# Two 32-head attentions: the queries of two heads from seven block products in place of eight

## The chip, the cores and the metric

The kernel is one program on one core of a Trainium2 chip (trn2). The metric is its time on the device in microseconds (us), lower is better. Engines: TensorE (PE, matrix products; PEld is its loading of weights), VectorE (DVE), ScalarE (ACT), GpSimd (POOL) and SyncE (SP, which issues the transfers here).

## The reference

A decoder of four layers on x of 16 batches by 64 tokens by 512 (1024 tokens in all), float32 throughout. The change touches the attention (`L3_attn`) and the cross attention (`L3_xattn`) of the last layer. Both have 32 heads of 128, in 8 groups of 4 heads that share a key and a value head:

```python
q = (hidden_states @ Wq.T).reshape(bsz, q_len, N_HEADS, HEAD_DIM).transpose(0, 2, 1, 3)   # L3_attn
q = q * cos + _rotate_half(q) * sin
q = (latents @ Wq).reshape(bsz, q_len, HEADS, HEAD_DIM).transpose(0, 2, 1, 3)             # L3_xattn
q = rms_norm(q, q_norm_w)
```

Then follow scores with the keys, softmax, the product with the values and the output product `@ Wo`, which is added to x. In `L3_attn` the scores are causal; in `L3_xattn` there are 128 keys per batch (64 of the context, 64 of the latents) and no mask.

## The kernel before, in words

The stages run one after the other; the last ones are `l2f`, `l3a` (`L3_attn`, kind "rope"), `l3x` (`L3_xattn`, kind "rms") and `l3f`. `l3a` and `l3x` are both built by `stage_gqa` (L600). The normalised tokens lie transposed in `kvT[:, k, 1, :]`: 128 features of block k (k = 0 to 3) by 1024 tokens. In `l3a` they are there when the stage begins; `l3x` makes them itself first (`front`). The half `kvT[:, k, 0, :]` held the context and is read by no one in these two stages.

**The work of a group.** Each stage goes through 8 groups of 4 heads. For each group TensorE makes: the keys (`keys`, L805, two blocks of 512 tokens, each 4 products of 128 by 128 weights with 512 tokens, summed over k in one bank of `pj`); the queries (`queries`, L812, 4 heads by 2 blocks, 4 products each, so 32); the scores of each head (`scores`, L864, 16 small products); transposes of the softmax's result (`turns`, L886); the values (`values`, L796, two blocks); the weighted values (`attend`, L901, four parts); and the output (`out`, L922, 8 tiles of 128 tokens with 4 products each). In the trace one float32 product stands as two records, so a product of 512 columns has two rows MATMUL 128x512. `l3x` also has, on TensorE, the sums of squares of keys (`key_sums`) and queries (`pair_sums` of two heads, `pair_turn`), for the rms norm.

**Banks and who empties them.** Keys, queries and values pass through the two banks of `pj`, by turns. In `l3a` ScalarE copies each block to `raw` (L988), and VectorE rotates it with four operations (`turn`, L1131 to L1145): a product with the cosine, two half-high products with the sine, and a sum into `qT` or `kT`. In `l3x` ScalarE squares the block (L1028) and copies it to `qT` (L1029); VectorE does nothing to queries. The softmax (`softmax`, L1167) is on VectorE, five large operations and a small one, with the exponential on ScalarE between (L1056). VectorE also adds each output tile to x (L1196).

**What sets the order.** Each engine has its own queue, written out by hand, and takes its instructions in that order; semaphores hold an instruction until its inputs are ready. The order is in `opening`, `group` and `closing` of each engine (TensorE: L939 to L979; ScalarE: L1071 to L1113; VectorE: L1242 to L1270). `group(n)` holds the queries of group n, from head 1 on, with the output of group n - 1 between them, and towards its end the keys and the first head's queries of group n + 1. `over_groups` (L698) writes TensorE's groups out one by one, and makes loops (`Fori`) of two groups on ScalarE and VectorE. SyncE loads weights of group n (`load`, L714) when the outputs of group n - 2 are done. GpSimd only copies key weights in `l3a` (L781), and helps in the norm of the next stage at the end. In `l3x` VectorE also unpacks weights of the next stage between the softmaxes (`unpack`, `dequantise`, L1199): part 0 is 32 small operations, part 1 four, and each later part two or three picks, a pick being L1224 and L1227. The first group does 8 parts, groups 1 to 6 four each, the last none.

## Time and profile before

| | us |
|---|---|
| median of 3 runs | 4217.38 |
| lowest and highest | 4216.12, 4219.28 |
| the profiled execution | 4217.35 |
| its span, first to last instruction | 4215.4 |
| mean granted clock of TensorE | 0.965 |
| `l3a`, first product to last group's last value block | 2714.0 to 3319.4 |
| `l3x`, the same | 3390.1 to 4094.8 |

A row of a timeline has the start in us from the span's start, the length, the engine, the line, the instruction and how many such in one go; in brackets is the idle time before it and what released it. Lengths of products are pipelined: the next one starts before the end that a row shows. A row of a group by line has the busy time, the mean of one in ns, and the idle time before it. Idle time of TensorE counts, since it is the engine that is nearly always busy; idle time of another one costs only where TensorE waits for it.

### The profile page before, as it was taken

Reading aid. Unit: us, or ns where it says so; the run is one execution under the profiler, and the core shown is the slowest. Engines: PE = TensorE matmul, PEld = TensorE weight load, DVE = VectorE, ACT = ScalarE, POOL = GpSimd, SP = SyncE. Lnnn points to the kernel's source line nnn. Section 1 sums busy time; section 2 is a strip of 40 time slices with the busy share of each in tenths; the row PEclk is TensorE's granted clock in tenths of the full one; section 3 lists DMA queues with packets and bytes.
Section 4 is the critical chain, followed back from the end, with each engine's and each line's share of the span. In section 5 each row is a group of like instructions: output and inputs, shape, how many; then the busy total and the mean of one; then the engine's idle time right before and its main releaser. Section 6 shows DMA issues by size and latency. Waiting matters only on the chain. (4 is left out here: it accounts for less than half of the span.)

```text
span 4215.4 us, 50580 instructions
## 1 busy us (share of the span) xinstructions
PE 3910.7 (93%) x18762; PEld 2088.9 (50%) x18762; DVE 2173.2 (52%) x3802; ACT 1425.1 (34%) x2570; POOL 313.7 (7%) x288
## 2 busy tenths in 40 slices
PE   8788989998989999998999889699999999999997
PEld 3333334554455555554447654355555455555554
DVE  0887765552247333333547548766556455444443
ACT  3777745553223211111113334222111133222332
POOL 1011001211001100000000111000000000000000
PEclk9899999999989999999999989899999999999998
DMA  5111121111100432311001022100010021111100
GB/s 187 45 40 35 53 76 33 33 31 58 40 33 16 178 113 103 116 54 73 1 13 55 1 101 58 64 21 21 21 40 21 1 67 36 36 35 40 65 6 23
DMA packets 133945, 215.20 MB, mean 51 GB/s; under 512 B 42576, under 2 KB 95056, under 8 KB 123104
## 3 DMA queue, kind: packets, MB, share of 16 engines
q1 hardware_dynamic: 133728, 212.19, 14.5%
q8 instruction: 151, 2.47, 0.2%
q14 instruction: 66, 0.54, 0.0%
HBM read 168.12 MB, written 44.04 MB: 50 GB/s over the span
## 5 line engine op out<-in xcount | busy, mean ns | idle before, releaser
L930 PE MATMUL l3a_po<-l3a_wo,l3a_cT 128*128 128x512 f32 x512 | 230.5, 603 | 3.5 <-ACT l3a_cT L1067 3.2
L436 PE MATMUL l1x_pj<-kvT,l1x_wq 128*128 128x512 f32 x512 | 228.3, 599 | 0.7 <-ACT kvT L240 0.7
L481 PE MATMUL l1x_po<-l1x_wo,l1x_cT 128*128 128x512 f32 x512 | 226.3, 596 | 1.2 <-issue 1.2
L819 PE MATMUL l3x_pj<-kvT,l3x_wq 128*128 128x512 f32 x512 | 225.5, 593 | 0.0
L819 PE MATMUL l3a_pj<-kvT,l3a_wq 128*128 128x512 f32 x512 | 224.9, 592 | 0.0
L577 DVE TENSOR_TENSOR x<-x,l1x_po 128x512 f32<-128x512 f32 x64 | 43.9, 687 | 267.1 <-PE l1x_po L481 267.1
L930 PEld LDWEIGHTS l3a_po<-l3a_wo,l3a_cT 128*128 128x128 f32 x512 | 95.5, 191 | 121.6 <-issue 110.9
L819 PEld LDWEIGHTS l3a_pj<-kvT,l3a_wq 128*128 128x128 f32 x512 | 95.5, 190 | 111.5 <-issue 111.4
L481 PEld LDWEIGHTS l1x_po<-l1x_wo,l1x_cT 128*128 128x128 f32 x512 | 95.7, 192 | 111.0 <-issue 111.0
L819 PEld LDWEIGHTS l3x_pj<-kvT,l3x_wq 128*128 128x128 f32 x512 | 95.5, 190 | 111.4 <-issue 111.4
L436 PEld LDWEIGHTS l1x_pj<-kvT,l1x_wq 128*128 128x128 f32 x512 | 94.6, 190 | 110.2 <-issue 107.2
L194 POOL TENSOR_TENSOR norm_rstd<-norm_half,minus_half 128x1 f32<-128x1 f32 x70 | 41.6, 595 | 1367.4 <-DVE norm_half L189 1367.4
L930 PE MATMUL l3x_po<-l3x_wo,l3x_cT 128*128 128x512 f32 x256 | 117.6, 603 | 0.7 <-issue 0.7
L1196 DVE TENSOR_TENSOR x<-x,l3a_po 128x512 f32<-128x512 f32 x56 | 38.4, 686 | 149.7 <-PE l3a_po L930 149.7
L930 PE MATMUL l3x_pc<-l3x_wo,l3x_cT 128*128 128x512 f32 x256 | 115.1, 592 | 0.0
L531 ACT COPY l1x_cT<-l1x_pa 128x512 f32<-128x512 f32 x64 | 34.4, 589 | 238.5 <-PE l1x_pa L470 238.5
L1631 ACT ACTIVATE l0a_signs<-l0a_lowest_a,l0a_scalars 128x1376 uint16<-128x1376 uint16 x68 | 98.0, 1442 | 47.9 <-DVE l0a_lowest_a L1755 47.1
L1740 DVE TENSOR_SCALAR_CACHE_REDUCE l0a_keep<-l0a_keep,l0a_scalars 128x1376 uint16<-128x1376 uint16 x64 | 105.3, 1646 | 3.2 <-DVE l0a_scalars L1746 1.1
L2627 PE MATMUL l1f_ph<-l1f_w,l1f_xT 128*128 128x448 f32 x256 | 104.6, 558 | 0.0
L2651 PE MATMUL l1f_po<-l1f_w,l1f_hT 128*128 128x512 f32 x224 | 101.6, 599 | 1.9 <-ACT l1f_hT L2694 1.9
L1740 DVE TENSOR_SCALAR_CACHE_REDUCE l0a_keep<-l0a_a,l0a_scalars 128x1376 uint16<-128x1376 uint16 x60 | 98.7, 1646 | 4.2 <-DVE l0a_scalars L1746 2.1
L1503 PE MATMUL l0a_pg<-kvT,fill_wk 128*128 128x512 f32 x160 | 74.5, 618 | 25.1 <-ACT l0a_s L1580 13.5
(532 smaller groups left out, 7633.7 us busy)
## 6 DMA issues: line engine op xcount, KB each, us to landing
l1x_kb<-l1x_keys SPq DMA_DIRECT2D x32, 512.0 KB, 4.7
l1x_vb<-l1x_values SPq DMA_DIRECT2D x32, 512.0 KB, 3.5
l1x_keys<-l0a_kv SPq DMA_DIRECT2D x40, 256.0 KB, 2.0
fill_wk<-in_L_xattn_Wk SPq DMA_DIRECT2D x8, 1024.0 KB, 5.7
kvT<-in_L_xattn_Wv SPq DMA_DIRECT2D x8, 1024.0 KB, 5.7
l1x_values<-l0a_kv SPq DMA_DIRECT2D x32, 256.0 KB, 2.3
l1x_wq<-in_L_xattn_Wq SPq DMA_DIRECT2D x8, 1024.0 KB, 5.0
l1x_sbias<-in_L_xattn_bias SPq DMA_DIRECT2D x8, 1024.0 KB, 6.8
```

The source lines that it names most:

```text
L194: self.nc.gpsimd.tensor_tensor(self.rstd[:, t:t + 1], self.half[:, t:t + 1], self.m.minus_half[:, 0:1], ALU.pow).then_inc(self.root_ready, 1)
L436: mm = pe.matmul(pj[:, j, :], wq[:, u, k, h * DH:(h + 1) * DH], m.kvT[:, k, 1, 512 * j:512 * (j + 1)], start=k == 0, stop=k == KC - 1)
L481: mm = pe.matmul(po[:, t % 2, :], cT[:, u, h, t * P:(t + 1) * P], wo[:, u, h, :], start=h == 0, stop=h == GH - 1)
L577: nc.vector.tensor_tensor(m.x[:, t, :], m.x[:, t, :], po[:, t % 2, :], ALU.add).then_inc(added, 1)
L819: mm = pe.matmul(pj[:, j, :], wq[:, u, k, h * DH:(h + 1) * DH], m.kvT[:, k, 1, 512 * j:512 * (j + 1)], start=k == 0, stop=k == KC - 1)
L930: mm = pe.matmul(outs[t % 2][:, :], cT[:, h, t * P:(t + 1) * P], wo[:, u, h, :], start=h == 0, stop=h == GH - 1)
L1196: nc.vector.tensor_tensor(m.x[:, t, :], m.x[:, t, :], outs[t % 2][:, :], ALU.add).then_inc(added, 1)
L1503: mm = pe.matmul(banks[b], wk[:, k, h * DH:(h + 1) * DH], m.kvT[:, k, 0, 512 * j:512 * (j + 1)], start=k == 0, stop=k == KC - 1)
L1631: ins = nc.scalar.activation(signs[:, :], words, ACT.Sign, bias=at[:, :], scale=-1.0, accum_out=total[:, :])
L1740: nc.vector.tensor_scalar(below, words, found[:, :], 0.0, ALU.is_lt, ALU.add, accum_out=cnt[:, :]).then_inc(link, step.next())
L2627: mm = pe.matmul(ph[:, c % 2, 0:CH1], f.xT[:, u, k, :], w1[:, k, c * CH1:(c + 1) * CH1], start=k == 0, stop=k == KC - 1)
L2651: mm = pe.matmul(f.po[:, :], hT[:, j, :], w2[:, j, :], start=j == 0, stop=j == HC1 - 1)
```

## The change

The queries of two heads (a pair p, two pairs per group) are a product of weights with blocks (features 0 to 255 and 256 to 511) by (head, head) and tokens with blocks (features) by (tokens 0 to 511, 512 to 1023). Before, this takes 8 block products, each of 2 products of 128 by 128 by 512. After, it takes 7 (`step` k = 1 to 7, 2 products each, 14 steps per group) and sums:

- **sums of tokens**, once per stage: four VectorE operations of 128 by 1024 (`fold_tokens`), into `kvT[:, i, 0, :]`.
- **sums of weights**, per pair: four GpSimd operations of 128 by 256 (`mix`), into `ws`; 8 per group, both stages.
- **sums of results**, per pair: ScalarE copies steps 1, 4 and 5 to SBUF (`saved`), VectorE adds steps 2, 3, 6 and 7 from the bank to something kept (`summed`), and three additions in SBUF (`join`, `join_both`) finish it, on GpSimd in `l3a` and on VectorE in `l3x`. In `l3x` ScalarE squares the finished blocks from SBUF (`square`) where it squared the bank.

The order is written anew: each step of two products alternates between the banks and waits for the bank's last reader; steps 1 to 6 of the first pair come ahead of the group that they belong to, and the steps of the second pair stand between parts of the output. VectorE's softmax is split into `scaled`, `shift` and `weighed`, with other work between; the last part of head 3 moves into the next group. In `l3x` VectorE unpacks four parts in each of the 8 groups: 4 parts fewer in the first, and 4 in the last, where there were none. All engines' groups are written out one by one, without loops.

```diff
-    NU = NV + NK + 8
+    NU = NV + NK
...
-        raw = st.sb("raw", [P, 2, 512])
+        raw = st.sb("raw", [P, 6 if rope else 2, 512])
+        ws = st.sb("ws", [P, 4, 2, DH])
...
+                def mix(n, p):
...
+                    if p == 0:
+                        pool.wait_ge(w_loaded[u], 8 * loads * (n + 2 - u))
+                        if n:
+                            pool.wait_ge(q_step, step_at(n - 1, 1, 6) + 2)
+                    else:
+                        pool.wait_ge(q_step, step_at(n, 0, 6) + 2)
+                    nc.gpsimd.tensor_tensor(ws[:, 0], low2, high2, ALU.add).then_inc(mixed, 1)
+                    pool.wait_ge(mixed, mixed_at(n, p, 0) + 2)
+                    nc.gpsimd.tensor_tensor(ws[:, 1], ws[:, 0], low, ALU.subtract).then_inc(mixed, 1)
+                    nc.gpsimd.tensor_tensor(ws[:, 2], low, low2, ALU.subtract).then_inc(mixed, 1)
+                    pool.wait_ge(mixed, mixed_at(n, p, 1) + 2)
+                    nc.gpsimd.tensor_tensor(ws[:, 3], high, ws[:, 1], ALU.subtract).then_inc(mixed, 1)
+                def join(n, p):
...
+                    nc.gpsimd.tensor_tensor(keep(1), keep(0), keep(1), ALU.add).then_inc(q_joined, 1)
...
+                    nc.gpsimd.tensor_tensor(keep(0), keep(0), keep(2), ALU.add).then_inc(q_joined, 1)
...
+                    nc.gpsimd.tensor_tensor(query(1, 1), keep(1), keep(2), ALU.add).then_inc(q_joined, 1)
...
+                    for c in range(2):
+                        block = wq[:, u, c if k == 1 else 2 + c, (2 * p + (k == 7)) * DH:(2 * p + (k == 7) + 1) * DH]
+                        weights = block if k in (1, 2, 7) else ws[:, {3: 1, 4: 0, 5: 2, 6: 3}[k], c, :]
+                        stream = {1: tokens(c, 0), 2: tokens(2 + c, 0), 3: fold(1, c), 4: fold(0, c), 5: fold(2, c),
+                                  6: tokens(2 + c, 1), 7: fold(3, c)}[k]
+                        mm = pe.matmul(pj[:, p if k % 2 else 1 - p, :], weights, stream, start=c == 0, stop=c == 1)
+                    mm.then_inc(q_step, 1)
```

TensorE's group, before and after (its waits: `values(0)` and `values(1)` of a group wait for `summed` of steps 6 and 7 of pair 1; `scores(n, u, 0)` in `l3a` waits for the rotation of block 1 of head 0, `scores(n, u, 1)` for that of head 1; the step after a step waits for its bank's reader):

```diff
                 def opening():
...
-                    queries(0, 0, 0)
+                    for k in range(1, 7):
+                        step(0, 0, 0, k)
...
-                    queries(n, u, 1)
+                    step(n, u, 1, 1)
+                    step(n, u, 0, 7)
                     scores(n, u, 0)
-                    pair_sums(n, 0)
                     if behind:
                         turns(n - 1, 3)
+                    pair_sums(n, 0)
+                    step(n, u, 1, 2)
                     pair_turn(n, 0)
-                    queries(n, u, 2)
+                    step(n, u, 1, 3)
                     if behind:
                         attend(n - 1, 0)
-                    scores(n, u, 1)
+                    step(n, u, 1, 4)
                     if behind:
...
-                        rest_of_out(n - 1, 1 - u)
+                        out(n - 1, 1 - u, 0)
+                        attend(n - 1, 1)
+                        out(n - 1, 1 - u, 1)
+                    scores(n, u, 1)
+                    step(n, u, 1, 5)
...
                     for j in range(NV):
                         values(n, u, j)
+                    pair_sums(n, 1)
                     turns(n, 0)
-                    queries(n, u, 3)
+                    pair_turn(n, 1)
                     scores(n, u, 2)
-                    pair_sums(n, 1)
                     turns(n, 1)
-                    pair_turn(n, 1)
                     if more:
                         all_keys(n + 1, 1 - u)
-                        queries(n + 1, 1 - u, 0)
+                        for k in range(1, 5):
+                            step(n + 1, 1 - u, 0, k)
                     scores(n, u, 3)
+                    if more:
+                        step(n + 1, 1 - u, 0, 5)
+                        step(n + 1, 1 - u, 0, 6)
                     turns(n, 2)
```

VectorE's order after (`add` in the parts named is of group n - 1, left out in the first group):

```diff
+                    fold_tokens()
                     all_keys(0, 0)
-                    queries(0, 0)
+                    summed(0, 0, 2)
+                    rotate(0, 0, 0)
+                    summed(0, 0, 3)
+                    join(0, 0)
+                    summed(0, 0, 6)
+                    join_both(0, 0)
+                    rotate(0, 0, 1)
...
+                    summed(n, 0, 7)
+                    rotate(n, 1, 1)
+                    summed(n, 1, 2)
+                    scaled(n, 0)
+                    summed(n, 1, 3)
+                    shift(0)
+                    rotate(n, 1, 0)
...
+                    weighed(n, 0)
+                    rotate(n, 2, 0)
...
+                    scaled(n, 1)
+                    join(n, 1)
+                    shift(1)
...
+                    join_both(n, 1)
+                    weighed(n, 1)
+                    summed(n, 1, 6)
+                    rotate(n, 3, 1)
...
+                    summed(n, 1, 7)
+                    rotate(n, 2, 1)
...
+                    rotate(n, 3, 0)
...
+                    for i in range(3):
+                        unpack(n, i)
+                    scaled(n, 2)
+                    shift(2)
+                    weighed(n, 2)
+                    unpack(n, 3)
                     if more:
                         all_keys(n + 1, 1 - u)
-                        queries(n + 1, 0)
-                    softmax(n, 3)
-                    unpack(lap, u, 3)
+                        summed(n + 1, 0, 2)
+                        rotate(n + 1, 0, 0)
+                        summed(n + 1, 0, 3)
+                    scaled(n, 3)
...
```

## Rows read from the trace of the kernel before

**Rows 1.** The page: span, and busy time of each engine.
```profile
span 4215.4 us, 50580 instructions
...
PE 3910.7 (93%) x18762; PEld 2088.9 (50%) x18762; DVE 2173.2 (52%) x3802; ACT 1425.1 (34%) x2570; POOL 313.7 (7%) x288
```

**Rows 2.** Stretches: from:to, length, busy us PE, PEld, DVE, ACT, POOL, clock, DMA, GB/s.
```profile
2722.60:2777.27 54.67, 54.67 (x301) 30.32 (x300) 44.29 (x68) 11.43 (x20) 1.70 (x2) 1.00 0.05 22
2945.00:3022.00 77.00, 76.15 (x375) 40.38 (x374) 43.86 (x67) 15.01 (x28) 1.00 (x1) 1.00 0.08 28
...
4102.00:4135.00 33.00, 20.88 (x121) 14.11 (x120) 12.54 (x12) 8.83 (x15) 0.00 (x0) 0.64 0.00 1
```

**Rows 3.** Groups by line: busy us, mean ns, then idle before and its releaser.
```profile
L819 PE MATMUL l3a_pj<-kvT,l3a_wq 128*128 128x512 f32 x512 | 224.9, 592 | 0.0
L930 PE MATMUL l3a_po<-l3a_wo,l3a_cT 128*128 128x512 f32 x494 | 222.8, 604 | 3.5 <-ACT l3a_cT L1067 3.2
...
L1224 DVE TENSOR_SCALAR l3x_pick<-l3x_code,l3x_lut 128x512 f32<-128x512 f32 x60 | 29.0, 484 | 4.4 <-DVE l3f_wl L1227 0.5
```

**Rows 4.** Timeline of TensorE, middle group of `l3a`: start, length, instruction, idle before.
```profile
2962.17 7.13 PE L930 MATMUL l3a_po<-l3a_wo,l3a_cT 128*128 128x512 f32 x16
...
2996.41 7.03 PE L819 MATMUL l3a_pj<-kvT,l3a_wq 128*128 128x512 f32 x16
```

**Rows 5.** Timeline of VectorE, `l3a`: rotation, softmax, rotation; addition from PSUM; two sine products twice.
```profile
2949.93 0.69 DVE L1139 TENSOR_TENSOR l3a_part<-l3a_raw,l3a_cosq 128x512 f32<-128x512 f32 x1 [0.19 <-DVE l3a_qT L1145]
...
2952.70 0.68 DVE L1175 SCALAR_TENSOR_TENSOR l3a_sc<-l3a_pS,causal 128x512 f32<-128x512 f32 x1
...
2957.09 0.68 DVE L1139 TENSOR_TENSOR l3a_part<-l3a_raw,l3a_cosq 128x512 f32<-128x512 f32 x1
...
2965.91 0.69 DVE L1196 TENSOR_TENSOR x<-x,l3a_po 128x512 f32<-128x512 f32 x1 [2.34 <-PE l3a_po L930]
...
3011.98 1.70 DVE L1142 TENSOR_TENSOR l3a_part<-l3a_raw,l3a_sink 64x512 f32<-64x512 f32 x2
...
3015.33 1.40 DVE L1142 TENSOR_TENSOR l3a_part<-l3a_raw,l3a_sink 64x512 f32<-64x512 f32 x2
```

**Rows 6.** Timeline of VectorE at the start of `l3a`.
```profile
2720.15 0.69 DVE L1139 TENSOR_TENSOR l3a_part<-l3a_raw,l3a_cosk 128x512 f32<-128x512 f32 x1 [11.78 <-ACT l3a_raw L988]
```

**Rows 7.** Timeline of TensorE, first group of `l3a`: its first value block.
```profile
2745.64 7.41 PE L802 MATMUL l3a_pj<-l3a_wvf,kvT 128*128 128x128 f32 x64
```

**Rows 8.** Timeline of VectorE, start of `l3x`: one softmax lies between these two.
```profile
3419.17 1.22 DVE L1179 TENSOR_TENSOR l3x_sc<-l3x_pS,l3x_rq 128x1024 f32<-128x1024 f32 x1 [16.54 <-ACT l3x_rq L1046]
...
3426.66 3.40 DVE L1207 TENSOR_SCALAR l3x_bits<-l3x_packed 128x64 int32<-128x64 int32 x32
```

**Rows 9.** Timeline of TensorE, start of `l3x`: first queries, first value block.
```profile
3399.96 13.90 PE L819 MATMUL l3x_pj<-kvT,l3x_wq 128*128 128x512 f32 x32
...
3427.31 7.41 PE L802 MATMUL l3x_pj<-l3x_wv,kvT 128*128 128x128 f32 x64
```

**Rows 10.** Timeline of TensorE, last group of `l3a`: first and last transposes.
```profile
3319.35 0.60 PE L897 MATMUL l3a_px<-ident,l3a_sc 128*128 128x128 f32 x4
...
3339.28 1.12 PE L897 MATMUL l3a_px<-ident,l3a_sc 128*128 128x128 f32 x4 [3.28 <-DVE l3a_sc L1191]
```

**Rows 11.** Timeline of TensorE, last group of `l3x`: first and last transposes.
```profile
4094.75 1.04 PE L897 MATMUL l3x_px<-ident,l3x_sc 128*128 128x128 f32 x8
...
4123.18 1.97 PE L897 MATMUL l3x_px<-ident,l3x_sc 128*128 128x128 f32 x8 [5.52 <-DVE l3x_sc L1191]
```

**Rows 12.** GpSimd, an addition of two tiles, by line.
```profile
L289 POOL TENSOR_TENSOR x<-x,l2a_ob 128x512 f32<-128x512 f32 x8 | 12.7, 1582 | 165.0 <-ACT l2a_ob L281 165.0
...
L289 POOL TENSOR_TENSOR x<-x,l1f_ob 128x512 f32<-128x512 f32 x8 | 10.1, 1268 | 218.3 <-ACT l1f_ob L281 218.3
```

**Rows 13.** Timeline of GpSimd, `l3a`: the same copy in two groups.
```profile
2930.72 0.62 POOL L781 COPY l3a_wk<-l3a_wkf 128x512 f32 x1 [79.99 <-PE l3a_pj L810]
3012.15 1.00 POOL L781 COPY l3a_wk<-l3a_wkf 128x512 f32 x1 [80.81 <-PE l3a_pj L810]
```

More of the change, by code:

```diff
@@ L979, in closing @@
                     rest_of_out(GROUPS - 1, 1)
-                over_groups(pe, opening, group, closing, unrolled=True)
+                over_groups(opening, group, closing)
             @block.scalar
@@ L1115, in _ @@
                 nc.scalar.preload_act_table_set("natural_log_exp_and_others")
-                over_groups(act, opening, group, closing)
+                over_groups(opening, group, closing)
             @block.vector
@@ new lines, in summed @@
+                def summed(n, p, k):
+                    dve.wait_ge(q_step, step_at(n, p, k) + 2)
+                    if k < 6:
+                        dve.wait_ge(q_saved, saved_at(n, p, 1) + 2)
+                    else:
+                        dve.wait_ge(q_joined, joined_at(n, p, "four" if k == 6 else "five") + 2)
+                    if k == 3:
+                        dve.wait_ge(q_summed, summed_at(n, p, 2) + 2)
+                    if rope and pair(n, p) and k != 3:
+                        dve.wait_ge(rotated, turn_q(n if p else n - 1, (1 if k == 7 else 0) + (0 if p else 2), 1 if k == 6 else 0) + 2)
+                    dst, src = {2: (query(0, 0), keep(0)), 3: (keep(0), keep(0)), 6: (query(0, 1), keep(1 if rope else 0)),
+                                7: (query(1, 0), keep(0 if rope else 1))}[k]
+                    nc.vector.tensor_tensor(dst, src, pj[:, p if k % 2 else 1 - p, :], ALU.add).then_inc(q_summed, 1)
@@ new lines, in rotate @@
+                def rotate(n, h, j):
+                    if rope:
+                        if h % 2 and j:
+                            dve.wait_ge(q_joined, joined_at(n, h // 2, "both") + 2)
+                        else:
+                            dve.wait_ge(q_summed, summed_at(n, h // 2, {(0, 0): 2, (0, 1): 6, (1, 0): 7}[h % 2, j]) + 2)
+                        if pair(n, h // 2):
+                            dve.wait_ge(s_ready, GH * n + h - 2 + 2)
+                        turn(turn_q(n, h, j), query(h, j), qT[:, h % 2, 512 * j:512 * (j + 1)], cosq, sinq)
@@ L1241, in opening @@
                 def opening():
+                    if rms:
+                        dve.wait_ge(front.copied, T + 1)
+                    fold_tokens()
                     all_keys(0, 0)
-                    queries(0, 0)
-                def group(n, u, behind, more, lap):
-                    chain.at(4 * TURN + per * n)
-                    queries(n, 1)
-                    softmax(n, 0)
-                    unpack(lap, u, 0)
-                    queries(n, 2)
-                    if behind:
-                        add(n - 1)
-                    softmax(n, 1)
-                    unpack(lap, u, 1)
-                    queries(n, 3)
-                    softmax(n, 2)
-                    unpack(lap, u, 2)
+                    summed(0, 0, 2)
@@ L1258, in group @@
                     if more:
                         all_keys(n + 1, 1 - u)
-                        queries(n + 1, 0)
-                    softmax(n, 3)
-                    unpack(lap, u, 3)
-                    assert chain.n == (per if more else per - 4 * TURN), (chain.n, per)
+                        summed(n + 1, 0, 2)
+                        rotate(n + 1, 0, 0)
+                        summed(n + 1, 0, 3)
+                    scaled(n, 3)
+                    if more:
+                        join(n + 1, 0)
@@ L1272, in closing @@
                     ahead.shifts(dve, T - 1, 0, T - 1)
-                over_groups(dve, opening, group, closing)
+                over_groups(opening, group, closing)
     ahead.done((T - 1, T))
```

357 lines of the change are left out of this document (245 added, 112 removed).

## The prediction

> **What bounds the kernel now.** I read the page first: TensorE is busy 93% of the span and no other engine over 52% [rows 1]. Then the stretches of the two changed stages. TensorE is busy for all of the first 54.7 us in `l3a`, and for 76.2 of 77.0 us of a middle stretch, at full granted clock, where VectorE has 43.9 us of work. In the first stretch VectorE has 44.3 of 54.7 us [rows 2]: that is 81%, since no output products stand beside its work there. By line, the queries of `l3a` are 512 records that never waited [rows 3]. So TensorE's own work sets the time, and an instruction of it that goes is worth its full price as long as the others keep up. The exceptions are the two ends, where the last softmaxes run with nothing beside them; one such stretch has TensorE busy 20.9 of 33 us at a mean clock of 0.64 [rows 2].
>
> All sums are against the profiled execution, 4217.35 us: a span of 4215.4 and 2.0 around it. The median of the runs is 4217.38, the same.
>
> **What goes.** 16 records of a query block last 7.03 us, of which some 0.16 is the last one's drain [rows 4]: 0.429 us each. A product of 512 columns is two records, 0.857 us. Per group 32 query products become 28, so 3.43 us go; over 16 groups 64 products, **54.9 us**. They do not go evenly: six steps in place of one head's queries are made ahead (10.3 us for 6.86, so 3.43 more in the opening), the seven groups after it save 3.43 each, and the last group, with nothing to make ahead, saves 6.86. Up to the last group's value blocks that is 20.6 us per stage; the rest is in the last group's end, worked out below.
>
> **What comes, and what covers it.**
> Hand-over of a bank: an output block of two units starts at 2962.17, its first unit of 8 records ends 3.43 later at 2965.60 [rows 4], and VectorE's addition from the bank starts at 2965.91 and takes 0.69 [rows 5]. So a bank is free again 0.3 + 0.7 + some 0.05 = 1.05 us after its step. The other bank's step takes 1.71. If the reader is idle, nothing is lost; what counts is whether VectorE's queue is late.
>
> Middle groups, `l3a`. VectorE gets 8 additions of 0.69 more, about 50 us of work in some 74. Where it could be late is the end of a group. A rotation takes 2.77 us and a whole softmax 4.39 [rows 5]. From the start of the keys (call it 0): key block 0 ends at 3.4 and is copied at 4.2, rotated until 7.1; block 1 is copied at 7.7 and rotated until 10.5; `summed` 2 until 11.2, the first rotation until 14.0, `summed` 3 until 14.7. TensorE wants bank for step 4 at 12.0 and for step 5 at 14.8 (steps 1 to 4 until 13.7, scores 1.1): just in time. Step 6 ends at 18.2, and the next user of its bank is step 1 of the next pair, with only 0.45 us of transposes between: it waits 1.05 - 0.45 = **0.6 us** per group, 4.2 in seven. In the middle of a group the outputs (3.43 us each) stand between steps and VectorE had idle stretches of 2 to 4 us before each addition: I cost the other hand-overs at nothing. Without that cover each would cost up to the 0.69 of its addition.
> Middle groups, `l3x`. The same place has 0.9 us of transposes, but `summed` 6 stands behind `scaled` 3 and two joins: 0.4 us, 2.8 in seven.
> An old wait goes: the outputs waited 3.2 us in `l3a` for ScalarE's copies [rows 3], which now have a step between; one of them, 1.1, is in the closing and stays. Gain 2.1.
>
> First group, `l3a`. Here nothing is beside VectorE. Its first rotation starts at 2720.15, after 11.8 us idle [rows 6]; the four sums of tokens (5 us, an estimate: twice 1024 columns' worth of the 0.69 for 512, less the fixed part) fit into that and cost nothing. From there to `summed` 6 of pair 1, which frees the bank for the first values, it has 7 rotations (19.6 with gaps), 7 additions from the bank (5.0), two softmaxes of which one exponential is now covered (8.1), and waits of 0.5 for key block 1 and 3.5 for step 6: 36.7 us, until 2756.9. TensorE would be there at 2745.64 [rows 7] + 3.43 (14 steps for 3 heads' queries) = 2749.1. Stall **8 us**; I take 8.2 with the hand-over. After it both go on as in a middle group.
>
> First group, `l3x`. `summed` 6 of the opening is late behind the joins: 1.2 us. Then the first `scaled` starts at 3419.17 [rows 8] plus two steps more (nine for two heads' queries, 1.7) plus 1.2 = 3422.1. From there VectorE has two softmaxes of 7.49 each [rows 8], `summed` 3 and 6 and two joins, four times 0.7: 17.8, until 3439.9. TensorE would be at the values at 3427.31 [rows 9] + 3.43 + 1.2 = 3431.9. Stall 8.0, with the other 1.2 and less the 0.7 us that it waited in the turning of sums before: **8.5**.
>
> Last group, `l3a`. From its first to its last transposes there are 19.9 us now [rows 10], of which 6.86 are queries. After: transposes 0.5, scores 1.1, and two softmaxes of 4.39 back to back: 10.5. Gain **9.4** (the queries' 6.86, and VectorE no longer behind the last rotations).
> Last group, `l3x`: 28.4 us now [rows 11]. After: 5.0 to 5.4 of transposes, sums and scores, two softmaxes 15.0, and the unpacking that now stands between them, two picks of 0.48 [rows 3] + 0.69: 2.4. That is 22.4 to 22.8; gain **6.0**.
>
> Clock. After the 3.2 and 5.5 us of idle in the last groups the same eight transposes took 1.97 us against 1.04 [rows 11], in the stretch with mean clock 0.64. That is the lower level of 1.2 GHz. The stalls in the first groups are of that size, and most of the time with a slow TensorE falls into the wait itself; I take 2 us for `l3a`, 3 for `l3x`, between 0 and 10 together.
>
> GpSimd. An addition of 512 columns there takes 1.27 to 1.58 us [rows 12]. The joins of `l3a` have 2.5 us each before someone waits, the weights' sums more; free. But they run beside VectorE: the key weights' copy took 1.00 us in one group and 0.62 in another [rows 13], and the two sine products beside the longer one took 1.70 us, against 1.40 [rows 5]. So 1 us of GpSimd costs VectorE some 0.3. Six joins and eight sums of weights (half the size) are some 14 us per group: VectorE loses 4 us, in its slack except in the first group, where I take 2. Bounds: 0, and 1 us for 1 us (rival 2).
>
> Written-out loops, more semaphores, ScalarE's three copies for four: nothing; TensorE's queue is written out already and its queries never waited [rows 3].
>
> **Sum.** `l3a`: -20.6 - 9.4 - 2.1 + 8.2 + 4.2 + 2 + 2 = -15.7. `l3x`: -20.6 - 6.0 + 8.5 + 2.8 + 3 = -12.3. Together -28.0: **4189.4 us**.
>
> **Rivals.**
> 1. All cover holds: the first groups don't stall (their waits overlap better than I chain them). Then 30.0 + 26.6 + 2.1 go: 4158.7. For it: VectorE was 19% idle in the first stretch [rows 2]. Against: its new work there, 7 additions and two more rotations before the values, is more than that idle. Chance 0.10.
> 2. GpSimd and VectorE share a path to memory. The trace has 0.3 us lost per us with a one-input copy; with two inputs on both sides it could be all of it. Then VectorE has 50 + 14 = 64 us in 74, the first group of `l3a` stalls some 8 us more, and each middle group 1 us: 28.0 - 8 - 7 + 2 saved are left, 15: about 4202. Chance 0.16.
> The Trainium skill, "GPSIMD Engine Reference", Specifications, has a rule that speaks for this: GpSimd's SBUF interfaces are shared with VectorE, with contention for VectorE instructions that have two SBUF inputs. Rotations are such. By that rule, taken as strict turn-taking, the time would be this rival's; the row's 0.3 us agrees with the rule in kind and is milder in size.
> 3. Slower: the chain at the end of a group, `summed` 2, rotation, `summed` 3, join, `summed` 6, before step 1 of the next pair. I found it in time by 0.1 us at step 5. If each of its links comes 0.5 us later, or a copy of ScalarE stands behind an exponential, TensorE waits twice or three times there. 28.0 us over 14 middle groups is 2.0 us per group, the point from which nothing is gained; at 4 us per group the time is 4217.35 + 28 = 4245. Against: ScalarE is busy 20% in these stretches [rows 2], and one late link eats only its own slack. Chance 0.07.
> 4. The forecast, with both first groups stalling 4 to 12 us each: 0.67.
>
> **How the numbers follow.** The likeliest case gives 4189.4. Its own bounds: no clock cost, no cost from GpSimd, half of the 16.7 us stalls, -15 in all; a clock cost of 10 and middle waits doubled, +12. With rival 2, and without most of rival 3 and of rival 1: **4168 to 4208**. A measurement of this kernel can tell about 0.2%, 8.4 us, from no change. Faster than 4208.9: the forecast, rival 1 and most of rival 2, 0.87. Within 8.4 us: 0.07. Slower than 4225.8: 0.06.
>
> **What would show it.** TensorE's query records: 896 in place of 1024, still 0.43 us each. In the first group of each stage, an idle time of TensorE before the first value block (line of `values`), released by VectorE's `summed`, 3 to 8 us. Before step 1 of pair 1, 0.4 to 0.6 us per group. Last transposes of `l3a` some 10.5 us, of `l3x` some 22.5 us after the first. The sine products of `l3a` longer than 0.70 us beside GpSimd. I am wrong if middle groups (77 us stretches) show TensorE idle by more than 2 us each, or if the first value blocks don't wait.

## The result and the profile after

The changed kernel takes 4209.64 us (median of 20 runs, 4206.61 to 4215.01), the kernel before beside it 4216.28 (20 runs, 4212.38 to 4219.28): a ratio of 0.9986, 95% interval 0.998 to 0.9993. It is faster by 6.6 us where 28 were forecast, and lies just outside the range of 4168 to 4208. The profiled execution took 4207.24 us.

The page of the changed kernel, span and first section, beside [rows 1]:
```profile
span 4205.3 us, 50002 instructions
...
PE 3867.1 (92%) x18634; PEld 2066.0 (49%) x18634; DVE 2328.0 (55%) x3986; ACT 1414.8 (34%) x2538; POOL 498.6 (12%) x464
```
The 128 records of the 64 products that go are gone (18762 to 18634). PE's busy time fell by 43.6 us and not by 54.9, so other records got longer. In the two first groups busy time is some 7 us longer than the products that went explain, at a granted clock of 0.92 where the kernel before has 0.96 and 1.00. In the groups behind them it is some 11 us longer at a granted clock of 1.00, so there it isn't the clock. (The tails and the other stages have some 7 us less.) Of the 43.6 us only some 10 arrived in the span of this execution. VectorE has 155 us more work, GpSimd 185.

The rest of the accounting is by start times in TensorE's timeline. A stage is cut at the first key block of its first group, of its second, and so on, and at the first and last transposes of the last softmaxes. Groups are counted from 0, so "keys 7" is the first key block of the last group. "Forecast" is the prediction's own sum put into these pieces: each group with 28 products for 32 is 3.43 shorter, and the last piece before the tail 3.43 longer, since no steps are left to make ahead.

| piece, us | before | after | change | forecast |
|---|---|---|---|---|
| `l3a`, first group (keys 0 to keys 1) | 47.90 | 58.59 | +10.7 | +8.8 |
| `l3a`, a middle group (six; mean before) | 80.96 | 79.69 | -1.3 | -3.1 |
| `l3a`, keys 7 to first last-group transposes | 71.7 | 77.57 | +5.9 | +3.7 |
| `l3a`, tail (first to last transposes) | 19.93 | 10.67 | -9.3 | -9.4 |
| `l3a`, all | 625.32 | 624.95 | **-0.4** | -15.7 |
| `l3x`, first group | 56.95 | 64.77 | +7.8 | +8.1 |
| `l3x`, a middle group (six) | 94.31 | 92.11 | -2.2 | -3.0 |
| `l3x`, keys 7 to transposes | 81.84 | 87.34 | +5.5 | +3.8 |
| `l3x`, tail | 28.42 | 21.44 | -7.0 | -6.0 |
| `l3x`, all | 733.1 | 726.19 | **-6.9** | -12.3 |

Both tails and the first group of `l3x` came as forecast, within 1 us. `l3a` as a whole gained nothing, and most of that is its middle groups. The two stages together gained 7.3 us, which agrees with the medians; the other 3 us between the two profiled executions lie ahead of `l3a`, where nothing was changed, and vary from run to run.

A middle group of `l3a`, end of the group before and start of its steps, in TensorE's timeline (start, length, engine, line, tiles, idle before and its releaser):
```profile
2784.28 3.70 PE L912 MATMUL l3a_pj<-kvT,l3a_ws 128*128 128x512 f32 x8
2787.82 0.60 PE L991 MATMUL l3a_px<-ident,l3a_sc 128*128 128x128 f32 x4
2788.76 3.70 PE L912 MATMUL l3a_pj<-kvT,l3a_wq 128*128 128x512 f32 x8 [0.34 <-DVE l3a_raw L1322]
2793.54 1.15 PE L977 MATMUL l3a_pS<-l3a_kT,l3a_qT 128*64 128x64 f32 x32 [1.08 <-DVE l3a_qT L1292]
2795.01 0.66 PE L991 MATMUL l3a_px<-ident,l3a_sc 128*128 128x128 f32 x4 [0.32 <-DVE l3a_sc L1390]
```
The first wait, 0.34, is the hand-over that was forecast (before `step` 1 of pair 1, behind `summed` 6). The second, 1.08, was not: the scores wait for the rotated queries of the first head. VectorE and GpSimd at that time:
```profile
2788.02 0.69 DVE L1322 TENSOR_TENSOR l3a_raw<-l3a_saves,l3a_pj 128x512 f32<-128x512 f32 x1 [1.48 <-PE l3a_pj L912]
2788.74 1.26 DVE L1286 TENSOR_TENSOR l3a_part<-l3a_raw,l3a_cosq 128x512 f32<-128x512 f32 x1
2790.03 2.23 DVE L1289 TENSOR_TENSOR l3a_part<-l3a_raw,l3a_sinq 64x512 f32<-64x512 f32 x2
2792.30 1.10 DVE L1292 TENSOR_TENSOR l3a_qT<-l3a_part 128x512 f32<-128x512 f32 x1
2793.32 0.67 DVE L1386 TENSOR_REDUCE l3a_tot<-l3a_sc 128x8 f32<-128x512 f32 x1
```
```profile
2788.19 1.27 POOL L828 TENSOR_TENSOR l3a_raw<-l3a_saves 128x512 f32<-128x512 f32 x1
2789.42 1.17 POOL L812 TENSOR_TENSOR l3a_ws<-l3a_wq 128x256 f32<-128x256 f32 x1
2790.66 1.06 POOL L814 TENSOR_TENSOR l3a_ws<-l3a_ws,l3a_wq 128x256 f32<-128x256 f32 x1
2791.69 1.17 POOL L815 TENSOR_TENSOR l3a_ws<-l3a_wq 128x256 f32<-128x256 f32 x1
2792.81 1.17 POOL L817 TENSOR_TENSOR l3a_ws<-l3a_wq,l3a_ws 128x256 f32<-128x256 f32 x1
```
A rotation of 2.77 us [rows 5] takes 4.6 here, beside GpSimd's last join and its weight sums. The addition before it, with one input in PSUM, and the reduction behind it, with a single input, keep their 0.69 and 0.67 beside the same engine.

The ends of these rows (start plus length) show how the two engines stand in each other's way. The join ends at 2789.46, the cosine product at 2790.00, the first weight sum at 2790.59; then the second weight sum at 2791.72, the sine products at 2792.26, the third weight sum at 2792.86, VectorE's sum at 2793.40 and the last weight sum at 2793.98. Each end is 0.54 to 0.60 us behind the one before it, which is the other engine's. The one step of 1.13 holds the first of the two sine products, whose own end the row doesn't show. So each instruction gets going only when the other engine's is done.

The first value blocks wait as forecast:
```profile
2747.85 1.90 PE L977 MATMUL l3a_pS<-l3a_kT,l3a_qT 128*64 128x64 f32 x32 [3.72 <-DVE l3a_qT L1292]
2758.58 8.85 PE L869 MATMUL l3a_pj<-l3a_wvf,kvT 128*128 128x128 f32 x64 [2.65 <-DVE l3a_raw L1322]
...
3436.47 9.50 PE L869 MATMUL l3x_pj<-l3x_wv,kvT 128*128 128x128 f32 x64 [7.95 <-DVE l3x_qT L1322]
```
Behind the waits the same 64 products take 8.85 and 9.50 us against the 7.41 of [rows 7], at a mean granted clock of 0.82 and 0.76: part of them ran at the lower level of 1.2 GHz.

### The profile page after: what moved, and what is told of

Its sections match the earlier page's. It is cut to its first block and busy times, and to the rows that moved or that the text cites. A ratio compares the mean times of both kernels' runs of the same rounds, so it can differ in the third digit from the quotient of the medians.

```text
span 4205.3 us, 50002 instructions
## 1 busy us (share of the span) xinstructions
PE 3867.1 (92%) x18634; PEld 2066.0 (49%) x18634; DVE 2328.0 (55%) x3986; ACT 1414.8 (34%) x2538; POOL 498.6 (12%) x464
## 5 line engine op out<-in xcount | busy, mean ns | idle before, releaser
L912 PE MATMUL l3a_pj<-kvT,l3a_ws 128*128 128x512 f32 x256 | 121.6, 608 | 1.8 <-DVE l3a_saves L1322 1.6
L912 PE MATMUL l3x_pj<-kvT,l3x_ws 128*128 128x512 f32 x256 | 119.4, 601 | 0.0
L2425 POOL TENSOR_TENSOR l0x_q<-l0x_q,l0x_qi 128x512 f32<-128x512 f32 x64 | 65.4, 1044 | 306.9 <-DVE l0x_qi L2713 306.9
L1289 DVE TENSOR_TENSOR l3a_part<-l3a_raw,l3a_sinq 64x512 f32<-64x512 f32 x128 | 96.3, 752 | 4.0
L1728 PE MATMUL l0a_pg<-l0a_wg,l0a_xT 128*128 128x512 f32 (+1 forms) x192 | 81.8, 585 | 16.1 <-issue 13.5
```

The source lines that it names most:

```text
L912: mm = pe.matmul(pj[:, p if k % 2 else 1 - p, :], weights, stream, start=c == 0, stop=c == 1)
L1289: nc.vector.tensor_tensor(batches(part[low:low + S, 1, :]), batches(src[high:high + S]), s, ALU.mult).then_inc(link, chain.next())
L1728: mm = pe.matmul(dst[:, c, 0:k], f.xT[:, n % 2, kc, :], w[:, kc, o:o + k], start=kc == 0, stop=kc == KC - 1)
L2425: nc.gpsimd.tensor_tensor(qv, qv, qi[:, c % 2, b, :].unsqueeze(2).to_broadcast([P, XH, XD]), ALU.mult).then_inc(q_done, 1)
```

## The experiments

Theory after the result: GpSimd's additions in `l3a` take from VectorE's two-input instructions just where those decide. Rivals: VectorE's own new work is too much, with or without GpSimd; or the cost is in TensorE's clock and in its seams, the places where it changes from products of one tile size to products of another, where no wait shows.

**One stage at a time.** `l3a`, then `l3x`, by the function of the kernel before:
```diff
-        stage_gqa(nc, m, "l3a", "rope", ...
+        stage_gqa_8(nc, m, "l3a", "rope", ...
```


> The kernel after with l3a as before (eight products), l3x as after. It splits the measured 6.6 us between the stages. By the account of the two traces l3a gained nothing (0.3 us from its first key product to its last output) and l3x gained 7 to 9: then this run is 7 us faster than before, 4209, the same as the changed kernel. Rival: both gained half, as the prediction had it in kind (15.7 and 12.3 of 28): then it is some 3 us faster than before, 4213.

> The kernel after with l3x as before, l3a as after. If l3a gained nothing, this is the time of before, 4216 within 2 us, and its l3a lasts 653 us from the first key product to the last output, as in both traces. Rival (equal shares): 3 us faster than before.

Measured: with the old `l3a` 4208.67 us (11 runs), ratio to before 0.9985, interval 0.9976 to 0.9994: as fast as the changed kernel. With the old `l3x` 4218.15 (11 runs), 1.0005, 0.9996 to 1.0014: no gain at all. So the whole gain is `l3x`'s, as the table says, and what `l3a` lost it lost inside itself.

**The weight sums taken out of the place where they stand.** `ws` gets two buffers in `l3a`, and both pairs' sums are made before the group:
```diff
-        ws = st.sb("ws", [P, 4, 2, DH])
+        ws = st.sb("ws", [P, 2 if rope else 1, 4, 2, DH])
...
-                    mix(n, 1)
+                    if rms:
+                        mix(n, 1)
...
                         mix(n + 1, 0)
+                        if rope:
+                            mix(n + 1, 1)
```


> In l3a the sums of weights get two buffers, and those of both pairs are made together before the group, when VectorE has little to do; l3x unchanged. Theory GpSimd (its work beside VectorE lengthens the rotation that scores 0 wait for): in the changed kernel the rotation beside three joins and four sums of weights took 5.1 us in place of 2.8. Without the sums beside it, its sine products go back from 2.23 to 1.4 and its last sum from 1.10 to 0.69, the wait of 1.08 us before scores 0 falls to under 0.2 and the 0.32 before the transposes goes: 1.2 us in each of 7 groups and 1 to 2 us in the first, 9 us, 4200. Theory seams (TensorE loses 0.1 us at each change between large and small products): nothing changes, 4209. Theory VectorE (too much work of its own): nothing in middle groups either, waits stay.

Measured: 4203.4 us (7 runs), ratio 0.9969, 0.9958 to 0.998. The last three middle groups took 78.46 to 78.50 us, 1.2 less. `l3a` in all took 619.39, 5.6 less than in the changed kernel, where the expectation had 9. The first group took 59.85, 1.3 more and not 1 to 2 less: it waits as long in all (10.2 us for 10.1), but more of it comes early, with the second pair's sums in the opening. The 8 records behind the wait for `summed` 3 took 5.37 us, at a granted clock of 0.68, for 3.67 at 1.00. (The rotation of 5.1 us in the expectation is 4.6 by the rows above, and one join runs beside it, not three.) The waits of TensorE between 2870 and 3270 us, in middle groups (waited for, us in total, times, longest), first of the changed kernel:
```profile
PE l3a_pS L977 <- DVE l3a_qT L1292: 5.4, 5, 1.1
PE l3a_pj L912 <- DVE l3a_raw L1322: 1.7, 5, 0.3
PE l3a_px L991 <- DVE l3a_sc L1390: 1.6, 5, 0.3
```
and of this experiment:
```profile
PE l3a_pj L918 <- DVE l3a_raw L1328: 2.1, 6, 0.3
PE l3a_px L997 <- DVE l3a_sc L1396: 1.2, 5, 0.2
PE l3a_pj L918 <- DVE l3a_saves L1328: 0.8, 2, 0.5
```
The same additions in another place: the wait of the scores is gone. That of the transposes fell only from 0.3 to 0.2. What counts is beside what GpSimd's work stands.

**The joins of `l3a` on VectorE.** 
```diff
-                    if rope:
-                        join(n, 0)
...
+                    dve.wait_ge(q_saved, saved_at(n, p, 5) + 2)
+                    dve.wait_ge(q_summed, summed_at(n, p, 3) + 2)
+                    nc.vector.tensor_tensor(keep(1), keep(0), keep(1), ALU.add)...
```


> In l3a the three joins of a pair go from GpSimd to VectorE, where l3x has them; the sums of weights stay on GpSimd as in the changed kernel. Theory GpSimd: the sums of weights start earlier, since they no longer stand behind the joins, but may still run beside the same rotation; the joins cost VectorE 6 x 0.7 us per group more. Step 1 of pair 1 waits for summed 6, which now stands behind two joins on VectorE: its wait grows from 0.34 to some 0.7 us, that of scores 0 falls from 1.08 to some 0.5. Together within 2 us of the changed kernel per stage, and the first group 2 us slower, as VectorE sets it: 4208 to 4212. Rival (joins were the costly part of GpSimd's work): waits before scores 0 vanish, 4202.

Measured: 4217.16 us (11 runs), ratio 1.0004, 0.9995 to 1.0013; a middle group 80.96. A miss, some 8 us slower than the changed kernel, and not the 4208 to 4212 that were expected. Its waits in the same stretch:
```profile
PE l3a_pj L909 <- DVE l3a_raw L1319: 8.5, 5, 1.7
PE l3a_pS L974 <- DVE l3a_qT L1289: 4.7, 5, 1.0
PE l3a_px L988 <- DVE l3a_sc L1387: 1.6, 5, 0.3
```
The wait before `step` 1 rose from 0.3 to 1.7, and not to 0.7: two joins of 0.69 now stand in VectorE's queue before `summed` 6. There the links of the chain are in series, and taking them off VectorE is right. The wait of the scores stayed, since the weight sums still stand beside the rotation.

**Nearly all of GpSimd's additions left out** in `l3a`. This kernel leaves out sums that the result needs; it only prices them.
```diff
+                cols = 1 if rope else DH
...
+                    low, high, low2, high2 = (w[:, :, 0:cols] for w in (low, high, low2, high2))
...
-                    nc.gpsimd.tensor_tensor(keep(1), keep(0), keep(1), ALU.add)
+                    nc.gpsimd.tensor_tensor(keep(1)[:, 0:1], keep(0)[:, 0:1], keep(1)[:, 0:1], ALU.add)
```


> In `l3a` GpSimd's weight sums and joins work on one column each, in the same order and behind the same waits; nearly all of these sums are left out. Theory (GpSimd's additions lengthen VectorE's turns beside them, and their own length makes the second head late): the wait before `scores` 0 goes (from 1.08 us per middle group to 0), VectorE's two longest turns fall from 2.23 to about 1.4 us and from 1.10 to 0.7, and a middle group of `l3a` takes 78.2 in place of 79.7. Rival (VectorE's own chain of copies, folds and sums is what is late, with or without GpSimd): the wait stays within 0.3 us of what it is and the group at 79.4 to 79.8. Second rival (the clock and the changes of shape take it): the same, with no wait to speak of at either place.

Measured: 4192.91 us (one run, so the readings are by start times in its trace). A middle group takes 77.94, the first group 53.74 (4.9 less), `l3a` in all 607.89, 17.1 less. The same place in VectorE's timeline:
```profile
2787.01 0.69 DVE L1331 TENSOR_TENSOR l3a_raw<-l3a_saves,l3a_pj 128x512 f32<-128x512 f32 x1 [1.48 <-PE l3a_pj L921]
2787.73 0.69 DVE L1295 TENSOR_TENSOR l3a_part<-l3a_raw,l3a_cosq 128x512 f32<-128x512 f32 x1
2788.45 1.40 DVE L1298 TENSOR_TENSOR l3a_part<-l3a_raw,l3a_sinq 64x512 f32<-64x512 f32 x2
2789.89 0.69 DVE L1301 TENSOR_TENSOR l3a_qT<-l3a_part 128x512 f32<-128x512 f32 x1
```
and in TensorE's:
```profile
2787.75 3.70 PE L921 MATMUL l3a_pj<-kvT,l3a_wq 128*128 128x512 f32 x8 [0.34 <-DVE l3a_raw L1331]
2791.38 1.15 PE L986 MATMUL l3a_pS<-l3a_kT,l3a_qT 128*64 128x64 f32 x32
```
The rotation is 2.8 us again and the scores don't wait, with all of VectorE's own new work still there: the first rival falls. The second falls as well: nothing in TensorE's order was changed, and what was missing came back. The hand-over's 0.34 stays, as it should: the one join that `summed` 6 needs was done 2.5 us before it in the changed kernel too.

**Only the weight sums left out**, in both stages (again sums that the result needs):
```diff
+                    low, high, low2, high2 = (w[:, :, 0:1] for w in (low, high, low2, high2))
+                    wt = ws[:, :, :, 0:1]
-                    nc.gpsimd.tensor_tensor(ws[:, 0], low2, high2, ALU.add)
+                    nc.gpsimd.tensor_tensor(wt[:, 0], low2, high2, ALU.add)
```


> In both stages the weight sums alone work on one column (nearly all of these sums are left out); the joins of `l3a` stay whole and on GpSimd. Of the 1.75 us that a middle group of `l3a` gained when all of GpSimd's additions shrank (79.69 to 77.94), theory (the weight sums beside VectorE's rotations and sums are most of it, as taking them out of that place gained 1.2): 78.3 to 78.6. Rival (the joins' own length, 1.27 us each in a chain, is most of it): 79.0 to 79.5. In `l3x`, where GpSimd has only the weight sums and no chain of its own, theory (its contention with VectorE is seen only at the wait before `step` 1, 0.33 us): 92.11 falls to 91.8; rival (it is hidden there): 92.11 as it is.

Measured: a middle group of `l3a` 78.49, of `l3x` 91.88 (4198.93 us, one run). So of the 1.75 us per group in `l3a` 1.20 are the weight sums' and 0.55 the joins'. In `l3x` the sums cost 0.23, but in another place than I expected: the 0.33 before `step` 1 stayed, and the 0.15 before `pair_sums` went, where TensorE waits for ScalarE's squares. In `l3a` the scores don't wait any more; TensorE waits for the hand-over and 0.28 us for the softmax before the transposes. VectorE's and GpSimd's rows at the rotation:
```profile
2788.14 1.27 DVE L1291 TENSOR_TENSOR l3a_part<-l3a_raw,l3a_cosq 128x512 f32<-128x512 f32 x1
2789.44 1.44 DVE L1294 TENSOR_TENSOR l3a_part<-l3a_raw,l3a_sinq 64x512 f32<-64x512 f32 x2
```
```profile
2788.81 0.65 POOL L815 TENSOR_TENSOR l3a_ws<-l3a_wq 128x2 f32<-128x2 f32 x1
2789.54 0.65 POOL L817 TENSOR_TENSOR l3a_ws<-l3a_ws,l3a_wq 128x2 f32<-128x2 f32 x1
2790.14 0.19 POOL L818 TENSOR_TENSOR l3a_ws<-l3a_wq 128x2 f32<-128x2 f32 x1
2790.29 0.64 POOL L820 TENSOR_TENSOR l3a_ws<-l3a_wq,l3a_ws 128x2 f32<-128x2 f32 x1
```
The cosine product beside the last join, which is whole here, still takes 1.27 us for 0.69. As far as the rows show, that is what the joins' 0.55 comes from: contention again, and not their own length in a chain. No run separates the two. A sum of two columns takes 0.19 us or 0.65: one that starts within a VectorE instruction ends just after it (2789.46 behind 2789.41, 2790.93 behind 2790.88).

**VectorE's order in the first group of `l3x`.** 
```diff
+                    first = rms and n == 0
+                    if first:
+                        join(n, 1)
+                        summed(n, 1, 6)
+                        join_both(n, 1)
+                        summed(n, 1, 7)
                     scaled(n, 1)
```


> In the first group of `l3x` the join, `summed` 6, the second join and `summed` 7 stand before the key scaling on VectorE, not behind it. Theory (the 8 us before `values` there are the order of VectorE's work alone, as the prediction had it): keys to keys in the first group falls from 64.8 to about 57, about that of the kernel before (56.95); program about 4201 to 4203. Rival (the wait moves to the next thing that VectorE is late with, the scores of that group, which want the scaled keys): 62 to 65, program within 0.1% of the changed kernel.

Measured: 4208.56 us (10 runs), ratio to before 0.9981, 0.9971 to 0.999. The first group took 58.56, 6.2 less, but the next 95.20, 3.1 more; the stage is 3.1 shorter, less than the timed runs can tell. The wait before the values fell from 7.95 to 0.55, so it was VectorE's order. So the first group came near the theory's 57, and half of it went in the next one, as the rival has it. The rows of what comes behind:
```profile
3430.47 7.41 PE L869 MATMUL l3x_pj<-l3x_wv,kvT 128*128 128x128 f32 x64 [0.55 <-DVE l3x_qT L1322]
...
3442.38 3.60 PE L977 MATMUL l3x_pS<-l3x_kT,l3x_qT 128*64 128x128 f32 x32
...
3454.55 1.13 PE L921 MATMUL l3x_pc<-l3x_qsq,l3x_ones 128*128 128x512 f32 x2 [0.67 <-ACT l3x_qsq L1131]
...
3463.11 3.67 PE L912 MATMUL l3x_pj<-kvT,l3x_ws 128*128 128x512 f32 x8 [1.90 <-ACT l3x_qT L1147]
```
The scores in between took 3.60 for their usual 1.97, at a granted clock of 0.53: nearly all at the lower level.

**The last unpacking behind the last softmax.** 
```diff
-                    unpack(n, 3)
+                    if more:
+                        unpack(n, 3)
...
                     weighed(GROUPS - 1, 3)
+                    unpack(GROUPS - 1, 3)
```


> The last sixteenths that VectorE unpacks in the last group of `l3x` are moved behind the last group's softmax. Theory (the wait before the last queries turn is VectorE's, which unpacks first): the tail of `l3x` falls from 21.44 to about 19.0, what follows the stage grows by less than 0.5; program 2 us less. Rival (the unpack is wanted right after the stage): the gain comes back as a wait in the stage behind, the program is the same.

Measured: tail 19.07, 2.37 less, and 0.2 less up to the end of the stage's outputs; the forecast had priced this unpacking at 2.4, and it is. But half of it came back in the next stage. Its first 8 records took 6.03 us, at a granted clock of 0.60, for 4.90 at 0.73 in the changed kernel, and from the last transposes to the last instruction there are 93.4 us for 92.2. All three traces with this move have these 93.4. The ten without it have 90.5 to 95.6, six of them 91.9 to 92.2, so this is likely and not certain. The program took 4208.41 us (10 runs), which alone can't show 2 us.

**`attend` 1 beside `scores` 1.** 
```diff
                         out(n - 1, 1 - u, 0)
-                        attend(n - 1, 1)
                         out(n - 1, 1 - u, 1)
+                        attend(n - 1, 1)
                     scores(n, u, 1)
```


> In both stages `attend` 1 stands right before `scores` 1, so that TensorE changes between its 512-column products and the small ones two times fewer in a group. Theory (each change of shape costs 0.1 us that no wait shows): a middle group of `l3a` takes 79.48 in place of 79.69, one of `l3x` is 0.1 to 0.2 shorter. Rival (what no wait shows is the drain behind waits, and a change of shape costs nothing): both within 0.05 of the changed kernel.

Measured (4212.05 us, one run, so again by start times): a middle group of `l3a` 79.49 to 79.51, 0.2 less, as expected; of `l3x` 92.11, not changed, where 0.1 to 0.2 less were expected. In `l3x` `attend` works on tiles of 128\*128 as the outputs do, in `l3a` on 64\*128. The seam in the changed kernel, and the same outputs in one piece:
```profile
2802.12 3.60 PE L1024 MATMUL l3a_po<-l3a_wo,l3a_cT 128*128 128x512 f32 x8
2805.65 1.13 PE L1011 MATMUL l3a_px<-l3a_pT,l3a_v 64*128 64x256 f32 x8
2806.71 3.70 PE L1024 MATMUL l3a_po<-l3a_wo,l3a_cT 128*128 128x512 f32 x8
2810.34 1.15 PE L977 MATMUL l3a_pS<-l3a_kT,l3a_qT 128*64 128x64 f32 x32
```
```profile
2804.38 7.03 PE L1024 MATMUL l3a_po<-l3a_wo,l3a_cT 128*128 128x512 f32 x16
```
Unit 0 takes 3.53 from start to start, unit 1 3.63, where a unit between two of its kind takes 3.43 [rows 4]: 0.1 us at each end of a run of 128\*128 products that meets another tile size. The change from 64\*128 to 128\*64 that the experiment puts in shows no such cost: `attend` 1 takes 1.06 from start to start either way. The Trainium skill, "TensorEngine Tiling (Array Packing)", Key Properties, says that changing the tiling mode drains TensorE; the traces agree where 128\*128 products are on one side, `l3x` by not changing; between the two smaller tile sizes no run here shows it.

**What paid, together.** Weight sums early, sums first in the first group of `l3x`, the last unpacking late, and `attend` 1 beside `scores` 1 in `l3a`:


> The moves that paid, together, joins on GpSimd: both pairs' weight sums made before the group (`l3a`, 5.3 us), sums before key scaling in the first group of `l3x` (2.9 to 3.1), the last unpacking behind the last softmax (2.4), `attend` 1 beside `scores` 1 in `l3a` (1.4). Theory (they are in different places and add up): 12 us under the changed kernel, about 4197. Rival (a gain in one place is given back in another, as 3.1 of 6.2 was): 4200 to 4204.

Measured: **4198.86 us** (5 runs, 4196.21 to 4203.39) against 4214.62 beside it (11 runs): 0.9963, 0.995 to 0.9977. `l3a` 617.72 and `l3x` 720.75, 7.2 and 5.4 less than in the changed kernel: within the stages the parts add up (12.7 of 12 expected). The medians of the whole program say 9 (by the two ratios to before) to 11; some 1.2 us are likely given back behind `l3x`, as above. It beats both kernels: the intervals of the two ratios to before (0.995 to 0.9977, and 0.998 to 0.9993) don't meet.

**And the first group of `l3a` in the order of `l3x`'s**, added to these:
```diff
-                    scores(n, u, 1)
+                    if not (rope and n == 0):
+                        scores(n, u, 1)
...
                     step(n, u, 1, 7)
+                    if rope and n == 0:
+                        scores(n, u, 1)
```


> As the three moves and `attend` 1, and in the first group of `l3a` too TensorE makes `step` 5 to 7 before `scores` 1 and VectorE the joins' sums `summed` 6 and 7 before it weighs the first head. Theory (the waits before the first values of `l3a`, 3.7 and 2.7 us, are the order of VectorE's work): the first group of `l3a` 3 to 4 us shorter than with the three moves, about 4194. Rival (VectorE has no spare time in that group, so the wait only moves on to the transposes): the same as with the three moves, within 1 us.

Measured: 4202.03 us (7 runs), 0.9968, 0.9957 to 0.998; `l3a` 617.75. The rival was right: the first group is 0.4 us shorter, which the next ones give back. Its waits in that group, scores and values, beside those of the kernel with the other moves:
```profile
PE l3a_pj L875 <- DVE l3a_raw L1334: 5.4, 1, 5.4
...
PE l3a_pS L983 <- DVE l3a_qT L1304: 1.2, 1, 1.2
```
```profile
PE l3a_pS L983 <- DVE l3a_qT L1301: 4.1, 1, 4.1
...
PE l3a_pj L875 <- DVE l3a_raw L1331: 2.3, 2, 1.3
```
6.6 us in one order, 6.4 in the other. In `l3a`'s first group VectorE has no time to spare, and order moves the wait without shortening it.

## Why the prediction was wrong, step by step

**What goes**: right. 448 query records per stage in place of 512, of 0.43 us. The old wait before the outputs of `l3a` is gone too.

**The step that failed**: "Six joins and eight sums of weights (half the size) are some 14 us per group: VectorE loses 4 us, in its slack except in the first group, where I take 2." The amount of contention was not too small. From keys to keys of one middle group (stretch, length, busy us of PE, PEld, DVE, ACT and POOL, then clock, DMA, GB/s), the changed kernel and the one with one-column sums:
```profile
2849.05:2928.74 79.69, 77.95 (x379) 40.94 (x377) 54.42 (x81) 14.61 (x26) 15.63 (x16) 1.00 0.07 27
```
```profile
2846.30:2924.25 77.95, 77.61 (x379) 40.89 (x378) 51.59 (x81) 14.54 (x26) 3.26 (x15) 1.00 0.07 28
```
The same 81 instructions of VectorE take 54.4 us against 51.6: 2.8 more, beside 12.4 us more of GpSimd (15.6 against 3.3), where I had 4 to 14. The word that failed is "slack". GpSimd's work is released by the same steps that release the rotation, so it stands beside the one rotation that TensorE is about to want, and 1.8 of the 2.8 us are lost there; they became 1.1 us of wait, behind which the softmax (0.3) was late as well. I had followed that chain with VectorE's undisturbed durations and found it in time by 0.1 us at `step` 5, and had not followed it to the scores. The two mechanisms that I had as separate rivals, 2 (contention) and 3 (the chain at the end of the group), work together in this wait: it goes when the sums stand elsewhere, and it goes when they are left out and the chain stays. Priced by the experiment with one-column sums, this step is 17.1 us and not 2. Without it `l3a` would have gained 17.4 us; the rest of my sum for `l3a` says 17.7. So for `l3a` this one term is all of the error in the total; in no piece of that trace is the rest of my sum off by more than 1 us.

**Hand-overs of a bank**: right in place; 0.34 idle in `l3a`, 0.5 by start times with the transposes' drain in it, forecast 0.6. In `l3x` 0.33 idle, or some 0.6 by start times, forecast 0.4: `step` 1 starts 0.5 late, and it and the step behind it take 3.63, where 3.53 is usual before a change of tile.

**"I cost the other hand-overs at nothing"**: right for the waits, but not for the seams. Steps put between outputs and small products meet them more often: a step of four records beside another tile size takes 1.82 and not 1.71. In a middle group 128\*128 products meet another tile size 12 times in `l3x`, 8 times in the kernel before; in `l3a` 16 times for 14. Of the 0.8 us per middle group by which `l3x` fell short, 0.23 are the weight sums and some 0.2 the hand-over; the rest, 0.3 to 0.4, is about what four more such places cost at 0.1 each. That is a reckoning from start times, without a run of its own for `l3x`.

**First groups**: `l3x` 7.95 and 1.2 waited, forecast 8.0 and 1.2. `l3a` 10.1 waited in six places, forecast 8.2 and 2 for GpSimd. With one-column sums 4.9 us of the group's length go: GpSimd's share was more than 2, and that of VectorE's own chain less than 8.2 (5.9 us waited). The rows behind the waits were 3.1 us longer in `l3a` and 2.1 in `l3x`, at the lower clock, where I had 2 and 3.

**Tails**: right, 10.67 for 10.5; 21.44 for 22.4 to 22.8, since one `pair_sums` of 1 us now stands ahead of the first transposes, in the piece before.

**Rivals.** The first (all cover holds) is out. The second had the right mechanism, and nearly the right price: 15 us in `l3a` in place of the 2 that I had in the sum, where 17.1 were measured. It put 8 of them in the first group and 1 in each other; they were 4.9 and 1.75. Its rule from the Trainium skill was right: two SBUF inputs on VectorE beside GpSimd. I had called the 0.3 us lost per us "milder", and misread the row: that copy takes 0.62 us by itself and was itself held up to 1.00 [rows 13], so the two engines took 0.3 and 0.4 from each other, as in taking turns. The third's place was right too: at the end of a group TensorE waits three times, 1.74 us together. Its point of decision for the whole program, 2.0 us in both stages, was not reached, since `l3x` waits 0.5 more than before. My own sign of being wrong, 2 us of idle in each middle group, was set too high: 1.74 and 1.47 were measured (0.4 and 1.0 before), and together with the seams that was enough to lose most of the gain.

## What to carry to other kernels

When work goes to GpSimd because it is idle, ask what VectorE does at the moment when that work is released, not how much slack VectorE has on the whole: a common trigger puts both on the critical path together. Follow the chain with the disturbed durations to the next instruction of the bounding engine that waits, and further than the first link that is just in time. Where the contended work can be made a group ahead at the price of a buffer, as the weight sums here, it is worth the buffer; where it is a link in a chain, moving it to VectorE can cost more than the contention.

## What the runs showed of the hardware

- GpSimd and VectorE take turns, instruction by instruction, when VectorE's has two inputs in SBUF, and both lose: VectorE's product of two SBUF tiles took 1.26 us for 0.69 beside a join, and a GpSimd weight sum of 256 columns 1.06 to 1.17 for the 0.73 that it takes alone, one of two columns 0.65 for 0.19. An addition of VectorE with one input in PSUM (0.69) and a reduction with one input in all (0.67) lost nothing, and GpSimd's join beside the former took 1.27, as elsewhere. "GPSIMD Engine Reference", Specifications, in the Trainium skill names the two-input case; the traces agree, and give it this size.
- 128\*128 products of 512 columns that meet another tile size (64\*128 or 128\*64) on TensorE take 0.1 us longer at each end, and no idle time shows it: 3.53 and 3.63 us for 3.43.
- A wait of 0.34 us idle moved the next start by 0.5 us in both stages (from the transposes to `step` 1 there are 0.94 and 1.37 us, for 0.43 and 0.87 without a wait): idle time leaves out the end of the record before it.
